# Codes to levels without a conversion: lines read the 32-bit codes

## The reference

```
x = x + mix0(x) @ ternary(w0) + b0
x = x + mix1(x) @ W.T + b1 + 4 * (mix1(x) @ lora_A.T) @ lora_B.T
W = NF4_LEVELS[q_weight] * q_scale      # codes 0..15 (int32), one scale per 64 inputs
```

## Time and profile before

| | us |
|---|---|
| median of 3 runs (364.3 to 364.63) | 364.47 |
| profiled execution, its time | 363.33 |
| profiled execution, its span | 361.5 |
| PE busy, share of the span | 352.1, 97% |
| DVE busy | 241.3, 67% |
| ACT busy | 170.4, 47% |
| POOL busy | 224.8, 62% |

### The profile page before, as it was taken

One profiled execution on the slowest core, in us unless ns is written; L12 is line 12 of the kernel. 1 busy time (PEld: TensorE's weight loads), 2 busy tenths in 40 slices (PEclk: granted clock), 3 DMA queues, 4 the chain that ended last, 5 costly groups with the idle time before them and its releaser, 6 DMA issues.

```text
span 361.5 us, 5526 instructions
## 1 busy us (share of the span) xinstructions
PE 352.1 (97%) x1832; PEld 298.5 (83%) x1832; DVE 241.3 (67%) x362; ACT 170.4 (47%) x302; POOL 224.8 (62%) x146
## 2 busy tenths in 40 slices
PE   6999999999999989999999999999999999999996
PEld 6788788788888878878888888888888888888884
DVE  3879968877997798874699878445263452634523
ACT  2976667978898788862142313313032130321300
POOL 0669999967876877859510220866367663676632
PEclk9999999999999999999999999999999999999999
DMA  7994401755264254413322320303315033150202
GB/s 226 324 287 135 162 29 30 285 188 180 92 204 156 97 170 158 170 62 120 127 107 69 123 95 24 118 0 125 116 61 181 1 123 118 60 180 2 116 31 87
DMA packets 27838, 44.63 MB, mean 123 GB/s; under 512 B 8834, under 2 KB 17026, under 8 KB 27810
## 3 DMA queue, kind: packets, MB, share of 16 engines
q1 hardware_dynamic: 26322, 43.69, 34.9%
q10 hardware_dynamic: 1488, 0.59, 0.7%
HBM read 27.49 MB, written 16.78 MB: 122 GB/s over the span
## 4 chain that ended last, share of the span: by engine, by line
PE 70%; DVE 10%; ACT 6%; issue 6%; POOL 5%; DMA 1%; SPq 0%; DVEq 0%; POOLq 0%; ACTq 0%
PE acc L1182 32%; PE acc L1144 23%; PE xT L1108 9%; PE spare L1108 3%; POOL x_first L551 3%; DVE hl L863 2%; ACT spare L714 2%; DVE W L912 1%; PE acc L1209 1%; DVE ys L892 1%; DVE side_p L906 1%; DMA mix<-in_L_cond_weights 1%; ACT hh L666 1%; ACT w_in L679 1%; DVE side_n L902 1%
## 5 line engine op out<-in xcount | busy, mean ns | idle before, releaser
L551 POOL TENSOR_TENSOR X<-X,bias 128x1024 f32<-128x1024 f32 x28 | 67.7, 2416 | 29.3 <-PE xT L1108 29.1
L1144 PE MATMUL acc<-T,hh 128*128 128x512 f32 x192 | 76.0, 396 | 0.0
L1144 PE MATMUL acc<-T,hl 128*128 128x512 f32 x192 | 75.0, 391 | 0.0
L714 ACT ACTIVATE spare<-q_mid 128x512 f32<-128x512 int8 x96 | 55.7, 596 | 18.1 <-DVE side_p L906 7.6
L1182 PE MATMUL acc<-W,hh 128*128 128x512 f32 x192 | 61.0, 389 | 0.0
L1008 DVE TENSOR_TENSOR X<-X,acc 128x512 f32<-128x512 f32 x36 | 24.8, 688 | 34.8 <-PE acc L1182 18.6
L1108 PEld LDWEIGHTS xT<-mix,X 128*128 128x128 f32 x352 | 42.6, 192 | 1.7 <-issue 0.3
L1108 PE MATMUL xT<-mix,X 128*128 128x128 f32 x352 | 42.9, 275 | 0.0
L1182 PEld LDWEIGHTS acc<-W,hh 128*128 128x128 f32 x192 | 36.0, 188 | 7.4
L1144 PEld LDWEIGHTS acc<-T,hl 128*128 128x128 f32 x192 | 36.1, 188 | 7.4
L610 POOL TENSOR_TENSOR X<-X,ys 128x512 f32<-128x512 f32 x18 | 22.6, 1286 | 31.1 <-DVE ys L997 31.1
(11 more groups left out here) (97 smaller groups left out, 657.7 us busy)
## 6 DMA issues: line engine op xcount, KB each, us to landing
out<-X SPq DMA_DIRECT2D x26, 512.0 KB, 2.7
X<-out SPq DMA_DIRECT2D x16, 512.0 KB, 3.4
X<-in_x SPq DMA_DIRECT2D x12, 512.0 KB, 3.4
q_raw<-in_L_ffn_q_weight SPq DMA_DIRECT2D x16, 256.0 KB, 3.0
w_in<-in_L_ffn_w SPq DMA_DIRECT2D x14, 256.0 KB, 6.0
x_first<-in_x SPq DMA_DIRECT2D x4, 512.0 KB, 5.4
out<-x_first SPq DMA_DIRECT2D x4, 512.0 KB, 5.0
out<-X SPq DMA_DIRECT2D x4, 256.0 KB, 2.0
```

Source lines behind the costliest of these rows:

```text
L551: pool.tensor_tensor(x_of(g), x_of(g), (bias1 if g >= NT else bias)[:, :], ALU.add).then_inc(s_xb, 1)
L714: act.activation(dst, q_mid[:, parity, :], ACT.Copy, scale=slope, bias=offset).then_inc(s_line, 1)
L1144: mm = pe.matmul(acc[:, bank_of(q), :], a[:, k, :], b, start=(k == 0 and j == 0), stop=(k == KB - 1 and j == len(terms) - 1))
```

## The change

The conversion into `q_mid` and its tile are gone. The eight lines of a piece read `q_raw` directly, the int32 codes 0 to 15, so each line's offset takes the code 7 in. `q_raw` gets three buffers instead of two, and its next load waits for all eight lines of the piece that used the buffer. The first line of a side would not hit its two levels exactly with one multiplication and one addition, so a third constant is added: DVE adds it in the first maximum (add, then max against the next line). The max against 0 moves to the second maximum, which thus becomes scalar_tensor_tensor. ACT's total for `share` becomes 8 x 16 = 128.

```diff
+    QS = 3
...
-        q_raw = sb("q_raw", [P, 2, HB, P], I32)
-        q_mid = sb("q_mid", [P, 2, BANK], I8)
+        q_raw = sb("q_raw", [P, QS, HB, P], I32)
...
             def load_q(d):
                 k, n = PIECES[d]
-                need(sp, s_qmid, d - 1)
-                sp.dma_start(q_raw[:, d % 2, :, :], q_v[n, k]).then_inc(s_qin[d % 2], 16)
+                need(sp, s_line, 2 * NL * (d - QS + 1))
+                sp.dma_start(q_raw[:, d % QS, :, :], q_v[n, k]).then_inc(s_qin[d % QS], 16)
...
             def lines(start, stop):
                 for u in range(start, stop):
-                    d, number = divmod(u, 2 * NL + 1)
-                    parity = d % 2
-                    number -= 1
-                    if number < 0:
-                        act.wait_ge(s_qin[parity], 16 * (d // 2 + 1))
-                        need(act, s_line, 2 * NL * (d - 1))
-                        act.activation(q_mid[:, parity, :],
-                                       q_raw[:, parity, :, :].rearrange("p o i -> p (o i)"), ACT.Copy,
-                                       bias=-float(NF4_ZERO)).then_inc(s_qmid, 1)
-                        continue
+                    d, number = divmod(u, 2 * NL)
                     sign, j = divmod(number, NL)
-                    slope, offset = (above, below)[sign][j]
+                    slope, offset = sides[sign][0][j]
                     if number == 0:
-                        act.wait_ge(s_qmid, d + 1)
+                        act.wait_ge(s_qin[d % QS], 16 * (d // QS + 1))
...
-                    act.activation(dst, q_mid[:, parity, :], ACT.Copy, scale=slope, bias=offset
-                                   ).then_inc(s_line, 1)
+                    act.activation(dst, q_raw[:, d % QS, :, :].rearrange("p o i -> p (o i)"), ACT.Copy,
+                                   scale=slope, bias=offset).then_inc(s_line, 1)
...
-            per = (2 * NL + 1) * ND
+            per = 2 * NL * ND
...
                     dve.wait_ge(s_line, 2 * NL * d + NL * sign + j + 2)
+                    if j > 0:
+                        dve.wait_ge(s_max, v)
                     if j == 0:
+                        ins = dve.scalar_tensor_tensor(dst, dst, sides[sign][1], spare[:, c % LR, :],
+                                                       ALU.add, ALU.max)
+                    elif j == 1:
                         ins = dve.scalar_tensor_tensor(dst, dst, 0.0, spare[:, c % LR, :],
                                                        ALU.max, ALU.max)
                     else:
-                        dve.wait_ge(s_max, v)
                         ins = dve.tensor_tensor(dst, dst, spare[:, c % LR, :], ALU.max)
```

More of the change, by code:

```diff
@@ L29 @@
 I32 = mybir.dt.int32
-I8 = mybir.dt.int8
 ALU = mybir.AluOpType
@@ L66, in nf4_lines, with first_line @@
 def nf4_lines():
-    lv = [np.float32(x) for x in NF4_LEVELS]
+    f = np.float32
+    lv = [f(x) for x in NF4_LEVELS]
     z = NF4_ZERO
-    above = [line_through(k, lv[z + k], k + 1, lv[z + k + 1]) for k in (1, 3, 5, 7)]
-    below = [line_through(-k, -lv[z - k], -k - 1, -lv[z - k - 1]) for k in (1, 3, 5)]
-    below.append((-0.5, 1.0 - 0.5 * z))
-    for q in range(16):
[L78 to L82, removed]
+    def first_line(a, b):
+        want = abs(lv[a]), abs(lv[b])
+        middle = (float(want[1]) - float(want[0])) / (b - a)
+        for i in range(-8, 9):
+            slope = f(middle + i * float(np.spacing(f(abs(middle)))))
+            offset = f(-a * float(slope))
+            add = f(float(want[0]) - (a * float(slope) + float(offset)))
+            if all(f(f(q * float(slope) + float(offset)) + add) == w for q, w in zip((a, b), want)):
+                return (float(slope), float(offset)), float(add)
+        raise ValueError("no such line")
+    sides = []
+    for way in (1, -1):
+        line, add = first_line(z + way, z + 2 * way)
+        lines = [line]
+        for k in (3, 5, 7):
+            a, b = z + way * k, z + way * (k + 1)
+            lines.append(line_through(a, abs(lv[a]), b, abs(lv[b])) if b >= 0 else (-0.5, 1.0))
+        sides.append((lines, add))
+    for q in range(16):
+        value = []
+        for lines, add in sides:
+            first, *others = (f(q * float(f(s)) + float(f(o))) for s, o in lines)
+            value.append(max(f(first + f(add)), *others, f(0)))
+        assert value[0] - value[1] == lv[q], q
+    return sides
 def build(nc, x, itok, mix0, w0, b0, mix1, q_weight, q_scale, b1, lora_a, lora_b, out):
@@ L122, in build @@
     assert C * 2 == P and NH == 2 and ND == NT and G == 16 and R == 8
-    above, below = nf4_lines()
+    sides = nf4_lines()
     x_v = x.rearrange("(t s) c f -> t (s c) f", s=2)
@@ L322, in build @@
         s_bin = sem("s_bin")
-        s_qin = [sem(f"s_qin{k}") for k in range(2)]
+        s_qin = [sem(f"s_qin{k}") for k in range(QS)]
         s_zero = sem("s_zero")
@@ L354, in build @@
         s_loraB = sem("s_loraB")
-        s_qmid = sem("s_qmid")
         s_line = sem("s_line")
```

## The result

| | before | after |
|---|---|---|
| median, us | 364.26 (6 runs, 364.16 to 364.63) | 361.22 (6 runs, 360.83 to 362.38) |
| ratio | | 0.9917, 95% interval 0.99 to 0.9935 |
| profiled execution, its span, us | 361.5 | 359.3 |
| `turn_w(0)` to `turn_w(15)`, us | 113.50 | 110.75 |

The kernel is faster by 3.04 us (2.4 to 3.6 by the interval); the forecast was 2.7. Measured again beside e5, the changed kernel had 360.74 against 363.80, 0.9911 (0.9893 to 0.9929).

The account below looks back on a forecast made before the run. PE was taken as the bound, with only its four waits in making the weight winnable: 0.73 + 1.19 + 0.40 + 0.56 = 2.88, less 0.2, gives 2.7 us. From 364.47 that forecast 361.8 us, range 361.1 to 364.0.

Parts of the forecast that it names:

- most 2.93 us: PE's four waits of `turn_w` for `low_w` while the weight is made: the most the change can gain, 2.93 us.
- The conversion's 9.9 us: 16 ACTIVATEs removed from ACT, 9.9 us, counted as at best about 0.5 us per place where ACT is late.
- int32 source: 128 ACT lines reading 4-byte instead of 1-byte codes: taken as 0, bounds -12 ns to nothing a line.
- Fourth gap: PE's wait at `turn_w(14)`, 162.90 us: closed with over 2 us of margin, worth 0.73 us.
- Second gap: PE's wait at `turn_w(4)`, 86.61 us: worth 0.40 us, or 0.28 if only the conversion's own time is won.
- First gap: PE's wait at `turn_w(2)`, 70.27 us: 0.56 of 0.61 us won, ACT's next `side_n` line held until POOL ends.
- Third gap: PE's wait at `turn_w(10)`, 132.16 us: closed with 0.1 to spare, worth 1.19 us or some tenths less.
- Loads of codes: `load_q` in SP's list, released one instruction (0.6 us) sooner: worth 0, nobody waits for it afterwards.
- the 0.2 taken off: Deduction from the 2.88 us sum, because removing a gap moves the next pair's inputs forward and the third has hardly a margin.
- Rival 1: Half of it: gaps with a short half or 0.1 margin shrink by one conversion only; 1.9 us, 362.3 to 363.4; chance 0.19.
- Rival 2: No change: waits between ACT and DVE through two `spare` buffers absorb the conversion's time; 364.1 to 364.6 us; chance 0.14.
- rival 3: Slower: ACT's 128 lines take 418 ns more each from int32 than int8; about 18 us, 382; chance 0.03.

Follow-up runs that it names:

- e5: Changed kernel with every line from half 9 on issued one place earlier in ACT's list; 360.49 us, ratio 0.9911 to the kernel before.
- e1: Kernel before with its 16 conversions kept, only ACT's lines spread as in the changed kernel; 362.41 us against 363.84, ratio 0.9968.
- e2: Changed kernel with the conversion's place in `share` left empty, so lines stand in their old halves; 362.52 us against 363.84 for the kernel before, ratio 0.9963.
- e7: e1 with loads of `x` ahead of loads of codes in SP's list, as in e3; 361.46 us against 363.80 for the kernel before, ratio 0.9933.
- e3: Kernel before with, for tiles 5 to 15, loads of codes behind the load of `x` in SP's list; 363.49 us against 363.84, ratio 0.9992.
- e4: Changed kernel with two code buffers instead of three; 394.49 us against 363.84 for the kernel before, ratio 1.0847.
- e8: e4 with loads of `x` ahead of loads of codes in SP's list, as in e3; 367.04 us against 363.80 for the kernel before, ratio 1.0086.
- e6: The changed kernel itself measured again, for comparison with e5; 360.74 us against 363.80 for the kernel before, ratio 0.9911.

## Why the prediction was right, step by step

- *PE is the bound, only its waits in the making of the weight can be won; most 2.93 us.* Right. Behind `turn_w(15)` nothing moved. The most was higher, 3.40 us (113.50 - 110.10): 0.28 of the difference is the late tile of `x`, which was not in my list, the rest some hundredths at each distance.
- *The conversion's 9.9 us are not path.* Right: ACT is busy 8.5 us less (170.4 to 161.9), PE won 2.75.
- *int32 source, second maximum as scalar_tensor_tensor: 0.* Right, by the rows above. What the prediction quotes from the Trainium skill (Vector Engine (DVE) Microarchitecture Reference, Points that are easy to get wrong) on two SBUF sources did not reach this case: the second source is in PSUM, and the row has 686 ns. No run here has both in SBUF.
- *Fourth gap 0.73 by order.* Right: 0.74, in e1 too, and none of it in e2.
- *Second gap 0.40.* Right: 0.43. Order closes all of it (e7), volume alone 0.27 (e2).
- *First gap 0.56 of 0.61, held by POOL.* The size is right (0.54, with 0.07 left), and either half of the change closes it (e1 0.50, e2 0.55). POOL does hold ACT there: the first line of `side_n` waits 0.59 us for it and begins at 66.61.
- *Third gap 1.19.* This term was mis-sized: 0.70. I let the second `high_x(12)` begin as soon as PE's transposes allow, 1.98 us after their start. After the change they start at 120.47. PE's rows and then ACT's:

```profile
120.47 1.95 PE L1119 MATMUL xT<-mix,X 128*128 128x128 f32 x16
...
125.91 0.60 PE L1220 MATMUL acc<-ident,side_p 128*128 128x128 f32 x4
...
130.75 0.63 PE L1220 MATMUL acc<-ident,side_p 128*128 128x128 f32 x4 [0.34 <-DVE W L923]
```

```profile
121.49 0.60 ACT L721 ACTIVATE spare<-q_raw 128x512 f32<-128x512 int32 x1 [0.73 <-DVE side_n L911]
122.03 0.61 ACT L721 ACTIVATE side_p<-q_raw 128x512 f32<-128x512 int32 x1
122.55 1.06 ACT L682 ACTIVATE hh<-xT 128x512 fp32r<-128x512 f32 x2
```

The second begins at about 123.03, 2.56 us after the transposes: ACT had waited 0.73 us for DVE to free a `spare` buffer, two instructions ahead. I had looked only at what PE allows and not at what stood in front on ACT itself. e5 moves the missing line out from behind `high_x`, and the gap is gone. By itself volume wins 0.52 here (e2) and order 0.03 (e1).
- *Loads of codes: 0, nobody waits.* This step was wrong. e3 shows 0.25 us in the kernel before. e1 against e7 shows 0.56 + 0.80 us as soon as PE comes sooner and the loads do not, so in the changed kernel the earlier release keeps open more than the 0.28 it seems to win. e4 shows 33. I had taken PE's table of waits for complete; it had no row for `mixed(10)`, because line 1211 just before it is drawn 0.48 us long and `mixed(10)` begins 0.49 us after it: the lateness is hidden under the drawn matmul. In e1, where it was longer, it stands in the table, put down to "issue". The release one instruction sooner, which the prediction did see, was worth something.
- *The sum.* 0.54 + 0.43 + 0.70 + 0.74 + 0.28 = 2.69, and some hundredths elsewhere make 2.75: 0.49 too much for the third gap was cancelled by 0.28 too little for the tile and by the 0.2 taken off for another reason. That the 2.7 agrees with 2.75 so closely is luck; the mechanism and three of the four gaps are not.

Rival 1 had the third gap's size (half a microsecond for one conversion, which e2 shows), but left most of the second gap standing, which closed whole. Its sum seems to have a slip: its 0.12 can only stand for the second gap, where the bullet on that gap says 0.28 if only the conversion's time is won; with 0.28 it would be 2.0. Rival 2 falls with e1 and e2, rival 3 with the rows.

## What to carry to other kernels

When an engine's list is spread over another's by a proportional count, taking an instruction out changes the order as well as the volume; here, of 2.75 us in the stretch, the change with the lines in their old places gave 1.58 (0.24 of them an earlier tile of `x`), and the order with a clear transfer queue gave 2.04 without removing anything (1.79 of them the order). The two don't add up, since the first gap and a part of the second are won by either. Count for each stretch what the consumer's last step needs and what the producer has issued by then: a shortfall of one puts everything that stands between, here another engine's output, onto the path. And look at the distance between fixed points of the bounding engine, not only at its table of waits, before calling a transfer queue free: a queue that nobody waits for now can be the next to be late when the waits ahead of it are gone.

## What the runs showed of the hardware that I had not expected

PE's waits in e8 and e4 cost more than their own length. In e8 PE sat idle for 3.7 us; the mean granted clock was 1.00 before that and 0.50, the lower of PE's two levels, from 85 to 88 us, and 1.7 us were lost on top. In e4 waits of 23.5 us came with another 9 us of slower matmuls. In the kernel before, whose waits in this stretch are 0.24 to 1.04 us long, the granted clock stayed at 1.00.

The first 20 us differ from run to run by more than most edits here. In the profile of the changed kernel PE waited 2.0 us for the first mix (1.6 before), and ran at a lower granted clock than before; two stretches of the changed kernel:

```profile
0.00:10.00 10.00, 6.48 (x34) 6.29 (x35) 3.32 (x6) 3.33 (x5) 0.70 (x6) 0.96 0.75 226
10.00:20.00 10.00, 10.00 (x64) 9.34 (x64) 9.44 (x16) 8.29 (x16) 7.47 (x6) 0.87 0.93 312
```

A mean of 0.87 means that PE was for a part of the ten us at the lower of its two levels, 1.2 GHz for 2.4. Before, both had 1.00. e2 and e7, which waited 2.3 and 2.4 us, had 0.91 to 0.92 in both stretches; e1, e3 and e5, which waited 1.4 to 1.6, had 1.00. `turn_w(0)` began at 55.39 to 57.12 us across the profiles of kernels whose work up to there is nearly the same; the latest, e6, had a clock of 1.00, so the clock is not the only cause, and what else it is was not followed.
